# State-space block of a two-layer decoder: three pairs of states summed on GpSimd ahead of the matmul, rows spread two states ahead

## The chip, the cores and the metric

The kernel is one program on one core of one Trainium2 chip. The time is device microseconds of one execution. In the engine names of the profile PE is TensorE (PEld its weight loads), DVE is VectorE, ACT is ScalarE, POOL is GpSimd and SP is SyncE.

## The reference, cut to what matters

The model is a decoder of two layers on an input x of 32 batches x 112 positions x 256 channels. Its first block, the one that is changed, is a state-space block (Mamba). Everything behind it (cross attention, switch layer, agent attention, a second cross attention, latent mixture) is untouched. Cut to its core, in float32:

```python
x_in, z = split(layernorm(x) @ W_in)                  # 512 inner channels each
xc = silu(causal_conv4(x_in) @ pw + conv_bias)        # 4 taps
low = xc @ W_x                                        # 16 ranks, 8 B rows, 8 C rows
delta = softplus(low[:16] @ W_dt + b_dt)
for n in range(8):                                    # 8 states for each inner channel
    h[n] = scan over time of  exp(delta * A[n]) * h[n] + delta * B[n] * xc
y = sum over n of C[n] * h[n]  +  xc * D
x = x + (y * silu(z)) @ W_out
```

The sum over n of the eight products C[n] * h[n], which the kernel calls read-outs, is what the change computes in another way.

## The kernel before

The block runs in `mamba_groups`. The 32 batches go in eight groups of four; T = 448 positions of a group lie side by side, and the 512 inner channels are IC = 4 chunks of 128 partitions, so that most operands of VectorE are 128 x 1792. `all_groups` runs group 0, then a hardware loop over groups 1 to 5, then group 6 and, with `final=True`, group 7. Each engine has its own `group(g, at, final)` that goes through the states n = 0 to 7 in an order written out by hand; semaphores tie the engines together. While the states of group g are scanned, TensorE and ScalarE prepare group g+1.

VectorE, for a state: `scan(n)` (L664, state n from decay and drive), `make_drive(n+1)` (L657, delta*inner times the B row), `make_read_out(n)` (L671, state times the C row, into `read_out[:, n % 2]`). At state 6 it also runs `add_to_x(g, 0)` (L687, adds the projected output in PSUM to x), at state 7 `statistics` (L695). Behind state 7 come `make_delta(g+1)` (L649, L651), `make_drive(g+1, 0)`, `add_to_x(g, 1)`, `statistics` and `finish(g)` (L679, four products of y in PSUM with the gates).

TensorE, for a state n: `spread(g, n+1)` (L452, two bf16 matmuls that copy the B and the C row of state n+1 onto all 128 partitions, in `row_bank[0]` and `row_bank[1]`, one PSUM bank each), then the step of that state, then `add_state(g, n)` (L464), which waits for the read-out of state n and adds it to the four `y_bank` accumulators by matmuls with the identity. The steps are: n = 0 `gate` (L415), `turn_rows` (L408), `skip` (L458); n = 1 to 4 `convolve` (L427) of one chunk; n = 5 `low_rank` (L437) and `project_out(g, 0)` (L475); n = 6 `deltas` (L446); n = 7 a wait for `split`, `spread(g+1, 0)` and `project_out(g, 1)`. A float32 matmul stands as two records in the trace, so that `add_state` and `skip` are 8 records, a `convolve` 16.

ScalarE, for a state n: `keep_rows(n+1)` (L591, copies both row banks into `rows[:, (n+1) % 2]`, once the read-out of state n-1 has been made), then at n = 0 `read_gates` (L545) and `read_rows` (L540), then `decays(n+2)` (L598, four exponentials, once the scan of state n is done), then at n = 2 and 4 `read_inner` (L551), n = 3 `normalise_rows` (L534), n = 5 `read_low` (L558), n = 6 `cast_first` (L565) and `softplus` (L576 to L584, with `cast_second`, L570, in its midst), n = 7 `keep_rows(g+1, 0)` and `decays` of states 0 and 1 of the next group.

GpSimd has one job in this block: `split_low(g+1)`, two subtractions a group (L380 on 64 x 448 and L382 on 32 x 448), which make the exact bf16 parts of the rows. The second waits for `cast_second`.

## Time and profile before

| what | us |
|---|---|
| median of three runs | 3070.16 |
| range of the three | 3066.61 to 3071.97 |
| the profiled execution | 3073.5 |
| its span | 3071.7 |
| mean granted TensorE clock | 0.928 |

The page of the profile gives the busy time of each engine over the whole span and, in 40 slices of 77 us, the busy share of each engine in tenths. The state-space block fills slices 2 to 10 (some 80 to 785 us). For single instructions the timeline is read: start, duration, engine, line, output and inputs, and in brackets how long the engine had been idle before the instruction and which instruction released it. Instructions of VectorE that follow each other without a wait overlap a little in these records: a 1792-column product recorded at 2.02 us is followed by the next one 1.94 us after its start, a scan recorded at 3.88 us after 3.80 us.

### The profile page before, as it was taken

To read this page: it belongs to the slowest core of one execution; us is meant where nothing else is said; L and a number is where in the kernel's file an instruction comes from. 1 tells how busy PE (TensorE), PEld (TensorE's weight loads), DVE (VectorE), ACT (ScalarE), POOL (GpSimd) and SP (SyncE) were. 2 spreads that over 40 slices of the span, in tenths; PEclk is the share of its full clock that TensorE was granted. 3 is DMA by queue.
4 is the path that set the end of the run, shared out by engine and by line. 5 is a ranking of instruction groups with operands and counts; after the bars stand their busy time and mean duration, and the time that the engine had idled before them with its cause. 6 is when DMAs were issued, how large, how long until landed. Compare 5 with 4: busy or idle time off the path is not lost. (4 is left out here: it accounts for less than half of the span.)

```text
span 3071.7 us, 60127 instructions
## 1 busy us (share of the span) xinstructions
PE 2722.0 (89%) x20702; PEld 1767.6 (58%) x20703; DVE 1997.4 (65%) x4542; ACT 1518.1 (49%) x2982; POOL 454.4 (15%) x482
## 2 busy tenths in 40 slices
PE   6899999996799999999876689999999799969993
PEld 3344444443466676766665347777777645556662
DVE  2588888888367777777555447777777555653334
ACT  2666666663156666666443136666666233302222
POOL 0000000000300000000033111000110032324441
PEclk9899999997899999999877789999999899969997
DMA  4000000000100000000000100000000120001225
GB/s 112 0 1 0 0 0 0 0 0 0 35 21 20 20 15 20 20 20 15 1 15 1 39 11 26 20 20 20 20 25 11 49 83 20 14 26 61 63 61 165
DMA packets 57938, 80.70 MB, mean 26 GB/s; under 512 B 8880, under 2 KB 47059, under 8 KB 57491
## 3 DMA queue, kind: packets, MB, share of 16 engines
q1 hardware_dynamic: 51778, 62.69, 7.2%
q0 software_dynamic: 6048, 16.52, 1.7%
q8 instruction: 71, 1.16, 0.2%
q14 instruction: 41, 0.33, 0.0%
HBM read 63.59 MB, written 15.60 MB: 26 GB/s over the span
## 5 line engine op out<-in xcount | busy, mean ns | idle before, releaser
L1120 DVE CUSTOM_DVE_ANT_0 xa_h_scores<-xa_h_score_bank,xa_h_added 112x375 f32<-112x375 f32 x1024 | 518.1, 544 | 148.5 <-PE xa_h_score_bank L1055 133.6
L1214 ACT ACTIVATE xa_h_probs<-xa_h_scores,xa_h_negmax 112x375 f32<-112x375 f32 x1024 | 561.4, 600 | 0.9 <-DVE xa_h_negmax L1127 0.6
L1067 PEld LDWEIGHTS xa_h_turn_bank<-keep_ident,xa_h_probs 112*125 112x125 f32 x3072 | 398.6, 190 | 91.4 <-DVE xa_h_probs_t L1134 22.2
L1067 PE MATMUL xa_h_turn_bank<-keep_ident,xa_h_probs 112*125 112x112 f32 x3072 | 438.5, 279 | 8.8 <-DVE xa_h_probs_t L1134 8.5
L1134 DVE COPY xa_h_probs_t<-xa_h_turn_bank 125x448 f32<-125x448 f32 x512 | 319.1, 623 | 150.9 <-PE xa_h_turn_bank L1067 137.6
L1220 ACT ACTIVATE xa_h_probs_t<-xa_h_turn_bank 125x448 f32<-125x448 f32 x256 | 138.6, 541 | 304.5 <-PE xa_h_turn_bank L1067 304.5
L464 PE MATMUL mb_y_bank<-mb_read_out,keep_ident 128*128 128x448 f32 x512 | 231.7, 601 | 30.3 <-DVE mb_read_out L671 30.3
L664 DVE TENSOR_TENSOR_SCAN mb_state<-mb_decay,mb_drive 128x1792 f32<-128x1792 f32 x64 | 253.8, 3965 | 0.2 <-ACT mb_decay L598 0.2
L1055 PE MATMUL xa_h_score_bank<-xa_h_keys,xa_h_queries 32*112 32x375 f32 x2048 | 231.6, 522 | 11.3 <-DVE xa_h_row_max L1120 10.7
L1080 PEld LDWEIGHTS xa_h_sums_bank<-xa_h_probs_t,xa_h_values 125*32 125x32 f32 x6144 | 141.9, 110 | 154.5 <-DVE xa_h_probs_t L1134 149.2
L1080 PE MATMUL xa_h_sums_bank<-xa_h_probs_t,xa_h_values 125*32 125x112 f32 x6144 | 202.7, 265 | 14.6 <-issue 7.3
L1033 PE MATMUL xa_h_proj_bank<-xa_context,keep_slot 128*128 128x375 f32 x512 | 190.5, 495 | 12.0 <-POOL xa_h_added L1016 5.3
L1038 PE MATMUL xa_h_proj_bank<-keep_slot,xa_context 128*125 128x256 f32 x768 | 196.8, 393 | 4.4 <-ACT xa_h_values L1203 1.4
L427 PE MATMUL mb_front_bank<-mb_normed_t,mb_w_eff 128*128 128x448 f32 x512 | 198.9, 541 | 0.7 <-ACT mb_normed_t L540 0.7
L657 DVE TENSOR_TENSOR mb_drive<-mb_delta_inner,mb_rows 128x1792 f32<-128x1792 f32 x64 | 129.4, 2022 | 94.7 <-ACT mb_rows L591 93.8
L464 PEld LDWEIGHTS mb_y_bank<-mb_read_out,keep_ident 128*128 128x128 f32 x512 | 106.9, 212 | 140.6 <-issue 98.3
L2350 ACT ACTIVATE lm_e_wide<-lm_e_turn_bank,lm_b 128x128 f32<-128x128 f32 x252 | 71.8, 368 | 185.6 <-PE lm_e_turn_bank L2299 185.6
L591 ACT ACTIVATE mb_rows<-mb_row_bank 128x448 f32<-128x448 f32 x128 | 62.2, 537 | 190.7 <-PE mb_row_bank L452 190.7
L1038 PEld LDWEIGHTS xa_h_proj_bank<-keep_slot,xa_context 128*125 128x125 f32 x768 | 137.2, 192 | 28.8 <-DVE xa_heads_out L1147 6.7
L598 ACT ACTIVATE mb_decay<-mb_delta,mb_decay_rate 128x444 f32<-128x444 f32 x256 | 148.2, 657 | 5.9 <-DVE mb_delta L649 5.7
L427 PEld LDWEIGHTS mb_front_bank<-mb_normed_t,mb_w_eff 128*128 128x128 f32 x512 | 97.0, 190 | 89.9 <-issue 86.2
L671 DVE TENSOR_TENSOR mb_read_out<-mb_state,mb_rows 128x1792 f32<-128x1792 f32 x64 | 135.5, 2117 | 0.1
(341 smaller groups left out, 4145.7 us busy)
## 6 DMA issues: line engine op xcount, KB each, us to landing
xa_context<-in_ctx_t SPq DMA_DIRECT2D x64, 375.0 KB, 3.1
lm_w<-in_m_w SPq DMA_DIRECT2D x16, 512.0 KB, 9.9
lm_e_wide<-lm_result_rows SPq DMA_DIRECT2D x8, 896.0 KB, 9.8
keep_x<-in_x SPq DMA_DIRECT2D x4, 896.0 KB, 16.0
lm_latent_rows<-lm_rows SPq DMA_DIRECT2D x8, 448.0 KB, 3.2
out_x<-keep_x SPq DMA_DIRECT2D x8, 448.0 KB, 6.3
xa_mask_raw<-in_key_mask SPq DMA_DIRECT2D x1, 1312.5 KB
mb_f_pw<-in_pw SPq DMA_DIRECT2D x1, 1024.0 KB
```

The source lines that it names most:

```text
L427: last = pe.matmul(by_batch(bank[:, 0:T]), w_eff[:, tap, c, m * 128:(m + 1) * 128], normed_t[:, c, :, tap:tap + S], start=tap == 0 and c = ...
L464: last = pe.matmul(y_bank[c][:, 0:T], keep.ident[:, :], read_out[:, n % 2, c, :], start=False, stop=n == N - 1)
L598: last = act.activation(decay[:, n % 2, c, :, 1:], by_batch(delta[:, c, :])[:, :, 1:], ACT.Exp, scale=decay_rate[:, c, n:n + 1])
L664: dve.tensor_tensor_scan(flat(state[:, n % 2, :, :]), decay[:, n % 2, :, :, :].rearrange("p c b s -> p (c b s)"), flat(drive[:, n % 2, :, ...
L1033: last = pe.matmul(proj_bank[:, 0:SK], wk[:, c, m * 128:(m + 1) * 128], context[1 - s][:, c, :], start=c == 0, stop=c == DC - 1)
L1038: last = pe.matmul(proj_bank[0:KP, j * D:(j + 1) * D], context[1 - s][:, c, kc * KP:(kc + 1) * KP], wv[:, c, :], start=c == 0, stop=c == D ...
L1055: last = pe.matmul(score_bank[g][0:S, 0:SK], queries[s][band, m, j, :], keys[s][band, m, :], start=True, stop=True)
L1067: last = pe.transpose(turn_bank[(par + kc) % 2][0:KP, g * S:(g + 1) * S], probs[par][:, g, kc * KP:(kc + 1) * KP], keep.ident[0:S, 0:S])
L1080: last = pe.matmul(sums_bank[32 * g:32 * (g + 1), c * S:(c + 1) * S], values[s][:, kc, G * c + g, :], probs_t[par][:, kc, g * S:(g + 1) * ...
L1120: dve.tensor_tensor_reduce(scores[par][:, g, :], score_bank[g][0:S, 0:SK], added[s][:, :], 1.0, -BIG, ALU.add, ALU.max, row_max[par][:, g: ...
L1134: dve.tensor_copy(probs_t[par][:, kc, :], turn_bank[(par + kc) % 2][0:KP, 0:T]).then_inc(turned_by_dve, 1)
L1214: act.activation(probs[par][:, g, :], scores[par][:, g, :], ACT.Exp, bias=negmax[s][:, G * c + g:G * c + g + 1]).then_inc(probs_ready, 1)
```

## The change

Read-outs of the states 0+1, 2+3 and 4+5 are added on GpSimd (`add_pair`), and only the sum of a pair is pushed through TensorE; the states 6 and 7 are pushed singly as before. `read_out` has three buffers in place of two; a sum takes the place of one of its two operands. TensorE pushes the pair sums at n = 2, 4 and 6, ahead of which it does the step of that state and a spread. Rows are spread two states ahead (`spread(g, n+2)` at n; states 0 and 1 of the next group at n = 7), and a spread stands behind the step of the state, not ahead of it. `skip` moves from n = 0 to n = 1, behind the first `convolve`. On ScalarE `read_low` moves ahead of `decays(7)`. On GpSimd the three additions of a group stand ahead of `split_low`.

```diff
--- before.py
+++ after.py
@@ -313,7 +313,7 @@
         delta, delta_inner = sb("delta", [128, IC, T]), sb("delta_inner", [128, IC, T])
         decay = sb("decay", [128, 2, IC, G, S])
         drive, state = sb("drive", [128, 2, IC, T]), sb("state", [128, 2, IC, T])
-        read_out = sb("read_out", [128, 2, IC, T])
+        read_out = sb("read_out", [128, 3, IC, T])
         gated_y = sb("gated_y", [128, IC, T])
         y_bank = [psum(f"y_bank{n}", [128, 512]) for n in range(IC)]
         front_bank = [psum(f"front_bank{n}", [128, 512]) for n in range(2)]
@@ -331,6 +331,11 @@
         decay_ready, drive_ready, state_ready, read_out_ready, summed = (
             sem(n) for n in ("decay_ready", "drive_ready", "state_ready", "read_out_ready", "summed"))
         skipped, gated, x_added = sem("skipped"), sem("gated"), sem("x_added")
+        pair_ready = sem("pair_ready")
+        PAIRS = 3
+        PUSHES = N - PAIRS
+        BUFFER = (0, 1, 2, 0, 1, 2, 0, 2)
+        SUM = (1, 0, 1)
         LOADED = mamba_w.count
 
         def slots(g):
@@ -381,7 +386,15 @@
                 pool.wait_ge(parts_cast, 2 * g + 2)
                 pool.tensor_tensor(low_parts[0:LOW, :], rest[0:LOW, :], low_parts[0:LOW, :], ALU.subtract).then_inc(split, 1)
 
+            def add_pair(g, k):
+
+                pool.wait_ge(read_out_ready, N * g + 2 * k + 2)
+                pool.tensor_tensor(read_out[:, SUM[k], :, :], read_out[:, BUFFER[2 * k], :, :], read_out[:, BUFFER[2 * k + 1], :, :],
+                                   ALU.add).then_inc(pair_ready, 1)
+
             def group(g, at, final=False):
+                for k in range(PAIRS):
+                    add_pair(g, k)
                 if not final:
                     split_low(g + 1)
 
@@ -458,11 +471,19 @@
                     last = pe.matmul(y_bank[c][:, 0:T], skip_diag[:, c, :], inner[:, c, :], start=True, stop=False)
                 last.then_inc(skipped, 1)
 
-            def add_state(g, n):
+            def push(held, stop):
+
+                for c in range(IC):
+                    last = pe.matmul(y_bank[c][:, 0:T], keep.ident[:, :], read_out[:, held, c, :], start=False, stop=stop)
+                last.then_inc(summed, 1)
+
+            def push_pair(g, k):
+                pe.wait_ge(pair_ready, PAIRS * g + k + 1)
+                push(SUM[k], False)
+
+            def push_state(g, n):
                 pe.wait_ge(read_out_ready, N * g + n + 1)
-                for c in range(IC):
-                    last = pe.matmul(y_bank[c][:, 0:T], keep.ident[:, :], read_out[:, n % 2, c, :], start=False, stop=n == N - 1)
-                last.then_inc(summed, 1)
+                push(BUFFER[n], n == N - 1)
 
             def project_out(g, half):
 
@@ -485,15 +506,14 @@
             def group(g, at, final=False):
                 first = at == 0
                 for n in range(N):
-                    if n + 1 < N:
-                        spread(g, n + 1)
                     if n == 0:
                         gate(g)
                         if not final:
                             turn_rows(g)
-                        skip(g)
                     if 1 <= n < 5 and not final:
                         convolve(g, n - 1)
+                    if n == 1:
+                        skip(g)
                     if n == 5:
                         if not final:
                             low_rank(g)
@@ -505,7 +525,14 @@
                             pe.wait_ge(split, 2 * (g + 2))
                             spread(g + 1, 0)
                         project_out(g, 1) if not first else pass_over(OUT_B)
-                    add_state(g, n)
+                        if not final:
+                            spread(g + 1, 1)
+                    if n + 2 < N:
+                        spread(g, n + 2)
+                    if n in (2, 4, 6):
+                        push_pair(g, n // 2 - 1)
+                    if n >= 2 * PAIRS:
+                        push_state(g, n)
 
             pe.wait_ge(loaded, LOADED)
             pe.wait_ge(setup, 1)
@@ -517,6 +544,7 @@
             deltas(-1)
             pe.wait_ge(split, 2)
             spread(0, 0)
+            spread(0, 1)
             all_groups(pe, group)
             project_out(GROUPS, 0)
             project_out(GROUPS, 1)
@@ -606,6 +634,8 @@
                         read_gates(g)
                         if not final:
                             read_rows(g)
+                    if n == 5 and not final:
+                        read_low(g)
                     if n + 2 < N:
                         decays(g, n + 2)
                     if final:
@@ -616,8 +646,6 @@
                         normalise_rows(g + 2)
                     if n == 4:
                         read_inner(g, (2, 3))
-                    if n == 5:
-                        read_low(g)
                     if n == 6:
                         cast_first(g)
                         softplus(g)
@@ -666,13 +694,16 @@
 
             def make_read_out(g, n):
                 dve.wait_ge(row_read[1], use_of_row(g, 1, n) + 1)
-                reuse(dve, summed, N * g + n - 1)
+                if n in (3, 5, 7):
+                    reuse(dve, pair_ready, PAIRS * g + n // 2)
+                else:
+                    reuse(dve, summed, PUSHES * g + {0: -1, 1: -2, 2: 0, 4: 1, 6: 2}[n])
                 dve.wait_ge(state_ready, N * g + n + 1)
-                dve.tensor_tensor(read_out[:, n % 2, :, :], state[:, n % 2, :, :],
+                dve.tensor_tensor(read_out[:, BUFFER[n], :, :], state[:, n % 2, :, :],
                                   rows[:, n % 2, 1, :].unsqueeze(1).broadcast_to([128, IC, T]), ALU.mult).then_inc(read_out_ready, 1)
 
             def finish(g):
-                dve.wait_ge(summed, N * (g + 1))
+                dve.wait_ge(summed, PUSHES * (g + 1))
                 dve.wait_ge(front_read[(GATES + 2) % 2], used(g, GATES + 2) + 1)
                 dve.wait_ge(front_read[(GATES + 3) % 2], used(g, GATES + 3) + 1)
                 for c in range(IC):
```

## Rows read from the trace of the kernel before

**Rows 1.** The page: busy us of each engine, share of the span, instructions.
```profile
PE 2722.0 (89%) x20702; PEld 1767.6 (58%) x20703; DVE 1997.4 (65%) x4542; ACT 1518.1 (49%) x2982; POOL 454.4 (15%) x482
```

**Rows 2.** Groups by line, 80 to 780 us: busy, mean ns, idle before, releaser.
```profile
L657 DVE TENSOR_TENSOR mb_drive<-mb_delta_inner,mb_rows 128x1792 f32<-128x1792 f32 x64 | 129.4, 2022 | 94.7 <-ACT mb_rows L591 93.8
...
L591 ACT ACTIVATE mb_rows<-mb_row_bank 128x448 f32<-128x448 f32 x128 | 62.2, 537 | 190.7 <-PE mb_row_bank L452 190.7
```

**Rows 3.** Timeline, all engines, group 3, states 1 to 3 (start us, us, what).
```profile
366.62 2.33 ACT L598 ACTIVATE mb_decay<-mb_delta,mb_decay_rate 128x444 f32<-128x444 f32 x4
...
370.98 0.98 ACT L591 ACTIVATE mb_rows<-mb_row_bank 128x448 f32<-128x448 f32 x2 [2.03 <-PE mb_row_bank L452]
371.56 2.02 DVE L657 TENSOR_TENSOR mb_drive<-mb_delta_inner,mb_rows 128x1792 f32<-128x1792 f32 x1 [3.57 <-ACT mb_rows L591]
...
376.99 3.17 PE L464 MATMUL mb_y_bank<-mb_read_out,keep_ident 128*128 128x448 f32 x8
...
380.37 6.18 PE L427 MATMUL mb_front_bank<-mb_normed_t,mb_w_eff 128*128 128x448 f32 x16
...
380.96 2.03 DVE L657 TENSOR_TENSOR mb_drive<-mb_delta_inner,mb_rows 128x1792 f32<-128x1792 f32 x1 [1.64 <-ACT mb_rows L591]
...
386.39 3.17 PE L464 MATMUL mb_y_bank<-mb_read_out,keep_ident 128*128 128x448 f32 x8
```

**Rows 4.** Timeline, VectorE: state 2 of groups 0, 6; state 3 of group 7.
```profile
122.92 2.03 DVE L657 TENSOR_TENSOR mb_drive<-mb_delta_inner,mb_rows 128x1792 f32<-128x1792 f32 x1 [6.53 <-ACT mb_rows L591]
...
623.52 2.02 DVE L657 TENSOR_TENSOR mb_drive<-mb_delta_inner,mb_rows 128x1792 f32<-128x1792 f32 x1 [0.61 <-ACT mb_rows L591]
...
715.82 2.03 DVE L657 TENSOR_TENSOR mb_drive<-mb_delta_inner,mb_rows 128x1792 f32<-128x1792 f32 x1 [2.69 <-ACT mb_rows L591]
```

**Rows 5.** Timeline, GpSimd and VectorE, group 0, states 6 and 7.
```profile
173.43 3.88 DVE L664 TENSOR_TENSOR_SCAN mb_state<-mb_decay,mb_drive 128x1792 f32<-128x1792 f32 x1
...
173.69 4.44 POOL L382 TENSOR_TENSOR mb_low_parts<-mb_rest,mb_low_parts 32x448 bf16<-32x448 f32 x1 [2.06 <-ACT mb_low_parts L570]
...
177.44 2.58 DVE L671 TENSOR_TENSOR mb_read_out<-mb_state,mb_rows 128x1792 f32<-128x1792 f32 x1
```

**Rows 6.** Timeline, all engines, group 3, states 6 and 7.
```profile
416.84 0.66 DVE L687 TENSOR_TENSOR keep_x<-mb_front_bank,keep_x 112x512 f32 x1
...
421.67 2.85 DVE L671 TENSOR_TENSOR mb_read_out<-mb_state,mb_rows 128x1792 f32<-128x1792 f32 x1
...
424.42 1.02 POOL L382 TENSOR_TENSOR mb_low_parts<-mb_rest,mb_low_parts 32x448 bf16<-32x448 f32 x1 [1.78 <-ACT mb_low_parts L570]
424.44 4.75 DVE L664 TENSOR_TENSOR_SCAN mb_state<-mb_decay,mb_drive 128x1792 f32<-128x1792 f32 x1
424.57 6.29 PE L464 MATMUL mb_y_bank<-mb_read_out,keep_ident 128*128 128x448 f32 x8 [0.84 <-DVE mb_read_out L671]
...
428.48 1.79 ACT L584 ACTIVATE mb_soft<-mb_soft,keep_one 128x1792 f32<-128x1792 f32 x1
...
431.68 2.01 DVE L649 TENSOR_TENSOR mb_delta<-mb_above,mb_soft 128x1792 f32<-128x1792 f32 x1
```

**Rows 7.** Timeline, VectorE and GpSimd in the last block of the kernel.
```profile
2721.14 2.29 DVE L2441 TENSOR_TENSOR lm_e_wide<-keep_slot 112x2048 f32<-112x2048 f32 x1
2723.34 2.88 DVE L2439 TENSOR_TENSOR lm_e_own_tile<-keep_slot 112x1008 f32<-112x1008 f32 x1
...
2721.37 3.78 POOL L2252 TENSOR_TENSOR lm_e_own_tile<-lm_e_own_tile,keep_slot 112x1008 f32<-112x1008 f32 x1 [37.23 <-DVE lm_e_own_tile L2439]
```

**Rows 8.** Groups by line, GpSimd, whole span: the largest two-operand additions.
```profile
L794 POOL TENSOR_TENSOR keep_x<-keep_x,xa_out_bias 112x1024 f32<-112x1024 f32 x16 | 37.9, 2371 | 236.4 <-ACT xa_out_bias L843 192.9 <-DVE xa_q_normed L64 43.4
```

**Rows 9.** Timeline: GpSimd beside a VectorE instruction with a PSUM operand.
```profile
869.17 0.93 POOL L990 TENSOR_TENSOR xa_h_queries<-xa_queries_t,keep_slot 128x448 f32<-128x448 f32 x1 [25.65 <-PE xa_h_score_bank L1055]
869.31 0.55 DVE L1120 CUSTOM_DVE_ANT_0 xa_h_scores<-xa_h_score_bank,xa_h_added 112x375 f32<-112x375 f32 x1 [0.42 <-PE xa_h_score_bank L1055]
```

**Rows 10.** Windows: length, busy of PE, PEld, DVE, ACT, POOL; granted clock, DMA.
```profile
340.00:342.00 2.00, 2.00 (x4) 0.77 (x4) 2.00 (x1) 1.91 (x2) 0.47 (x1) 0.50 0.00 0
```

## The prediction

> **What bounds the kernel now.** I read the page first: TensorE is busy 89% of the span and VectorE 65% [rows 1], but that is a mean over stages, so the groups by line of the state-space block alone come next, and then the timeline of one group of it, engine by engine. In the block VectorE is the engine whose idle time means something. Its scans, drives and read-outs fill nearly all of it, and almost all that it waits for is one thing: the drive of the next state waits for the rows that ScalarE copies, 93.8 us in total, and ScalarE in turn has waited 190.7 us for the spread on TensorE [rows 2]. The timeline shows why. In states 2 to 5 TensorE pushes the read-out, spreads, and convolves without a break, and the next push starts 9.40 us after the last one (376.99 to 386.39); the push and the spread are 3.38 us of that (376.99 to 380.37), the convolution 6.02 (380.37 to 386.39) [rows 3]. VectorE needs only 3.80 + 1.94 + 1.93 = 7.67 us for a state, as consecutive starts go, and waits the rest, 1.64 us as recorded (1.73 with the overlap of records) [rows 3]. So TensorE's order sets the pace of four to five states, by its work and because a spread stands behind a push, and VectorE that of everything else.
>
> **What goes: pushes.** Three of eight pushes go. At some 3.0 us each (3.38 less some 0.38 for two bf16 matmuls of one pass) that is 9.0 us of TensorE's work a group. Two states then cost it 2 x 6.02 for convolutions, 3.0 for a push and 0.8 for spreads, 15.8 us, where VectorE needs 2 x 7.67 = 15.3 before anything is added. Alone, this would make the two about equal.
>
> **What goes: waits for rows.** A spread two states ahead is issued when the row bank has been read, which is as soon as read-out n-1 is made. ScalarE then copies (0.98 us) while the scan of 3.88 us runs, so the drive finds its rows. The recorded waits are 93.8 us over 47 drives; each is 0.09 more in true pace, 97.8 in total. One kind stays in part. At state 2 the copy also stands behind `decays(2)` on ScalarE, which ended at 368.95, while the copy began at 370.98: only 2.03 of that wait of 3.57 goes, because ScalarE is held by the gates before [rows 3]. Groups 2 to 5 keep 1.6 each, group 0 keeps 4.5 of its 6.53, while groups 1, 6 (0.61) and 7 have less than 2 to lose and lose it [rows 4]. That leaves 11.2. Removed: 97.8 - 11.2 = 86.6 us. What is late next is no longer rows but the port, below.
>
> **What comes: three additions a group on GpSimd, and who pays.** No addition of 128 x 1792 stands in the trace. The nearest is 112 x 1024 at 2.37 us (2.35 undisturbed) [rows 8], which is 2.29 ns a column; the 448-column one takes 1.02 us [rows 6], 2.28 ns. Both point at 1792 x 2.29 = 4.1 us. A price by the columns alone cannot be under 3.7 (0.93 x 4, from the cheaper form with a broadcast operand [rows 9]), nor do I see a reason for more than 4.4. GpSimd has time for it. But it doesn't work beside VectorE: in the trace the two exclude each other whenever VectorE's instruction has two SBUF operands. A GpSimd subtraction of 1.02 us issued just after a scan took 4.44 and ended only after the scan, which kept its 3.88; the read-out behind it grew from 2.02 to 2.58 [rows 5]. Where GpSimd came first, the scan grew from 3.88 to 4.75 and, two instructions before, the read-out from 2.02 to 2.85 [rows 6]. So VectorE loses what GpSimd takes, less some 0.17 us of start-up. It holds for a longer GpSimd instruction too: one that had to wait from 2721.37 to 2723.43 and then ran for 1.72 made VectorE's next one 2.88 us, where 1008 columns at the pace of 2.02 for 1792 would be 1.14 [rows 7]. An addition is released when the second read-out of its pair is made; by then the next scan holds the port, so the addition runs at the scan's end and the next drive waits for it. Price: 24 additions x (4.11 - 0.17) = 94.6 us.
>
> The Trainium skill ("SBUF — State Buffer", Who interferes with whom) says the same as a rule: a VectorE instruction with two SBUF inputs and a GpSimd instruction that reads SBUF take the shared port for a whole instruction, and the other blocks. It speaks against this change, and by that rule the trace agrees, as far as 1.7 us long ones show it. Its figure for a two-input addition of 2048 fp32 columns on GpSimd ("GPSIMD Engine Reference", Performance versus the Vector engine, 4497 ns) would give an estimate of 3.93 us for 1792, and a sum 4 us lower than mine.
>
> One part of the additions is covered: `add_to_x(g, 0)` at state 6 reads PSUM, and such an instruction isn't held up (0.55 us beside a running GpSimd product, its usual length) [rows 9]. It fits under the third addition in groups 1 to 7: 7 x 0.58 = 4.1 us given back [rows 6]. Without that cover the sum is 4.1 higher.
>
> **Moved steps, costed at nothing.** `split_low` is queued behind the third addition on GpSimd. Its L380 then gets the port behind drive 7, L382 behind the read-out of state 6; each delays VectorE by about 0.85 as now. `cast_second` on ScalarE waits for L380, and behind it are a quarter of the softplus, Exp and Ln. I follow it by VectorE's clock: Ln ends 2.4 us before `make_delta` is due; before, it ended at 430.27 with `make_delta` at 431.68, 1.4 us ahead [rows 6]. `skip` behind the first convolution fills time in which TensorE is not awaited. `read_low` ahead of `decays(7)` costs the scan of state 7 nothing, as there are two states of lead. The waits of read-outs 3, 5 and 7 for the addition two states back, and of read-out 4 for the first push (some 18 us earlier), end early. `finish` waits for the last push, which has the same work ahead of it as now. In group 7 the same account holds: drives there wait 2.69 [rows 4].
>
> **The sum.** -86.6 + 94.6 - 4.1 = +3.9 us. The span of 3071.7 becomes 3075.6, the profiled execution's 3073.5 becomes 3077.4. That execution lies 3.3 above the median of 3070.16; on the median's scale the forecast is 3074. Seen for one group: from the drive at 371.56 to that at 623.52 three groups pass, the last of them shorter by 3.57 - 0.61 of waiting, so a group takes (251.96 + 2.96) / 3 = 85.0 [rows 3, 4]. Less its waits for rows (3.66, four of 1.73, 2.28: 12.9) and 1.7 for `split_low`, VectorE's own pace is 70.4. Afterwards: 70.4 + 1.7 + 1.65 (state 2) + 3 x 3.94 - 0.6 = 85.0 again. The gain of TensorE and the loss of VectorE cancel. The bounds of an addition, 3.7 and 4.4, move the sum by -10 and +7.
>
> **The rivals.** (a) The port is shared more kindly in long instructions, or additions hide: if VectorE lost nothing, 3070 - 87 = 2983. For it speaks only that no addition of 4 us has been seen; against it every collision in the trace. A milder form has the gates step at the full clock in all groups, so that the 11.2 us that stay go too: 3063. Together 0.13.
> (b) The softplus chain becomes late (slower): `cast_second` waits for L380, which waits for the third addition and a drive. If L380 gets its turn one instruction later (the read-out, 1.9 us) and TensorE's `deltas` are late as well, Ln ends behind the read-out of state 7, and VectorE waits before `make_delta`. The point is 2.4 us of lateness; 1.5 to 2.5 us beyond it in seven groups is +10 to +17, so about 3088. The slack of 1.4 us of today speaks for it, the order of the port (who waits gets it next) against. 0.12.
> (c) TensorE's clock. It now waits some 3 us ahead of each push of a pair. After waits of this kind its granted clock is 0.50, the 1.2 GHz level [rows 10], and a push takes 6.29 in place of 3.17 [rows 6]. It has 19.3 - 15.8 = 3.5 us to spare in two states, so it becomes the bound once over 7 us of each 19.3 run at half speed; the stretches of now are under that. At 10 us it costs 1.5 us in each of 21 pairs, 3105. 0.06.
> (d) The change doesn't do what it says: rows still come late, and the 94.6 are added alone, 3160. ScalarE's 2.03 us of idleness ahead of the copy, until TensorE, speaks against [rows 3]. 0.03.
>
> **How the numbers follow.** The forecast case has 0.66 and its own range is 3062 to 3085. About 0.2%, 6 us, is what a measurement of this kernel can tell from no change. Within the case the sum lies inside 3064 to 3076 with 0.46, above with 0.15, below with 0.05. With (a) 0.13 faster, (b) 0.12, (c) 0.06 and (d) 0.03 slower, and rounding (a)'s milder form partly into "same": faster 0.17, same 0.47, slower 0.36. The range takes in the bounds of the addition and most of (b): 3060 to 3092.
>
> **What would show it.** The additions stand on GpSimd with about 4.1 us of their own, recorded at up to 8 as they wait for a scan. The drive behind scans 2, 4 and 6 takes some 6 us in place of 2.02, with no idle time before it. Drives of states 3 to 7 wait for no rows; that of state 2 waits some 1.6 in groups 2 to 5. A group still takes 85 us. TensorE's busy time falls by up to 70 us, with more of it at 0.50. I am wrong if drives keep their 2.02 us (then it is much faster), if `make_delta` stands behind a wait for Ln, or if `finish` waits for a push.

## The result, and the profile after

| | us |
|---|---|
| changed kernel, median of 10 runs | 3060.26 (3059.38 to 3067.24) |
| kernel before, 10 runs | 3070.51 (3064.97 to 3073.68) |
| ratio, with its 95% interval | 0.9972 (0.9963 to 0.9981) |
| profiled execution after, its span | 3060.0, 3057.6 |

The changed kernel is faster by 10 us, 0.28%, where the forecast was 3.9 us slower. The page of the changed kernel first; its columns are those of [rows 1]:

```profile
PE 2667.0 (87%) x20510; PEld 1736.8 (57%) x20511; DVE 2078.2 (68%) x4542; ACT 1519.2 (50%) x2982; POOL 644.4 (21%) x506
```

TensorE has 55 us less work, VectorE is recorded busy 81 us longer with the same number of instructions, and GpSimd has the 24 additions. The groups by line, changed kernel, 80 to 780 us (busy, mean ns, idle before, releaser), answer to [rows 2]:

```profile
L685 DVE TENSOR_TENSOR mb_drive<-mb_delta_inner,mb_rows 128x1792 f32<-128x1792 f32 x64 | 213.6, 3338 | 15.5 <-ACT mb_rows L619 14.7
L392 POOL TENSOR_TENSOR mb_read_out<-mb_read_out 128x1792 f32<-128x1792 f32 x24 | 179.7, 7489 | 446.7 <-DVE mb_read_out L702 446.7
L619 ACT ACTIVATE mb_rows<-mb_row_bank 128x448 f32<-128x448 f32 x128 | 61.7, 532 | 79.7 <-DVE mb_read_out L702 32.3 <-issue 26.6 <-PE mb_row_bank L465 20.8
```

The drive's idle time has fallen from 94.7 to 15.5 us, and its busy time has grown from 129.4 to 213.6: two numbers of nearly the same size with opposite signs. In the timeline of group 3, states 1 to 4, the exchange is seen in one place (changed kernel; VectorE and GpSimd; answers to [rows 3]):

```profile
371.36 2.03 DVE L685 TENSOR_TENSOR mb_drive<-mb_delta_inner,mb_rows 128x1792 f32<-128x1792 f32 x1 [2.56 <-ACT mb_rows L619]
...
375.24 3.88 DVE L692 TENSOR_TENSOR_SCAN mb_state<-mb_decay,mb_drive 128x1792 f32<-128x1792 f32 x1
...
375.40 7.50 POOL L392 TENSOR_TENSOR mb_read_out<-mb_read_out 128x1792 f32<-128x1792 f32 x1 [34.12 <-DVE mb_read_out L702]
...
379.04 5.74 DVE L685 TENSOR_TENSOR mb_drive<-mb_delta_inner,mb_rows 128x1792 f32<-128x1792 f32 x1
...
390.44 1.99 DVE L685 TENSOR_TENSOR mb_drive<-mb_delta_inner,mb_rows 128x1792 f32<-128x1792 f32 x1
```

The addition begins 0.16 us into the scan, ends at 382.90, 3.78 us after the scan's end at 379.12, and the drive behind the scan is recorded at 5.74 us in place of 2.02. The drive of the next state, with no addition beside it, has 1.99 and no wait for rows. At states 6 and 7 of the same group (changed kernel, VectorE and ScalarE; answers to [rows 6]):

```profile
417.14 0.66 DVE L718 TENSOR_TENSOR keep_x<-mb_front_bank,keep_x 112x512 f32 x1
417.72 5.14 DVE L685 TENSOR_TENSOR mb_drive<-mb_delta_inner,mb_rows 128x1792 f32<-128x1792 f32 x1
422.78 2.85 DVE L702 TENSOR_TENSOR mb_read_out<-mb_state,mb_rows 128x1792 f32<-128x1792 f32 x1
425.55 4.72 DVE L692 TENSOR_TENSOR_SCAN mb_state<-mb_decay,mb_drive 128x1792 f32<-128x1792 f32 x1
...
428.49 1.79 ACT L612 ACTIVATE mb_soft<-mb_soft,keep_one 128x1792 f32<-128x1792 f32 x1
...
432.76 2.01 DVE L677 TENSOR_TENSOR mb_delta<-mb_above,mb_soft 128x1792 f32<-128x1792 f32 x1
```

`add_to_x` is hidden under the third addition, and Ln ends at 430.28, 2.48 us ahead of `make_delta`.

So the block does what the forecast said, and it gains nothing. The first scan starts at 104.3 us (before: 104.9), and the statistics' aggregation right behind the block (its first instruction outside) at 785.5 (before: 785.8; second profiles of both kernels, below, have it at 787.3 and 784.5, so the block's length is known to some 3 us). The 14.1 us by which the two profiled spans differ are 0.3 up to there and 13.8 behind it, in blocks that the change doesn't touch. Cut by the first instructions of each block in the timelines:

| stretch behind the block | before | after |
|---|---|---|
| up to the first attention's heads | 56.2 | 56.2 |
| its 8 heads | 664.5 | 660.0 |
| its output projection | 46.3 | 45.0 |
| agent attention | 245.3 | 243.9 |
| second attention: heads, output | 650.3 | 650.4 |
| latent attention | 260.4 | 255.3 |
| last block | 362.9 | 361.4 |

Two things make these differences. The first is a stall of TensorE in the latent attention that has no releaser. In the timeline it stands ahead of one pair of products, in the kernel before:

```profile
2580.65 0.70 PE L1915 MATMUL lm_a_query_banks<-lm_a_keys_wide,lm_a_queries 32*112 32x448 f32 x2 [3.75 <-issue]
```

and in the changed kernel at the same product:

```profile
2569.63 0.63 PE L1946 MATMUL lm_a_query_banks<-lm_a_keys_wide,lm_a_queries 32*112 32x448 f32 x2 [0.39 <-issue]
```

The second is TensorE's granted clock. The windows of the first heads have the same instructions in both kernels but another busy time of TensorE (length; busy of PE, PEld, DVE, ACT, POOL; granted clock, DMA); first the kernel before:

```profile
842.00:1506.50 664.50, 635.50 (x6592) 454.49 (x6593) 469.82 (x1507) 412.14 (x865) 50.35 (x64) 0.98 0.06 18
```

then the changed kernel:

```profile
841.70:1501.60 659.90, 630.04 (x6592) 450.52 (x6592) 469.80 (x1507) 412.42 (x865) 50.46 (x64) 0.99 0.06 18
```

Most of the 5.5 us of busy time lie at the end of the stretch, as the timeline shows. In the kernel before the last turns of a head run at half speed, with the clock at its 1.2 GHz level:

```profile
1491.64 0.84 PE L1080 MATMUL xa_h_sums_bank<-xa_h_probs_t,xa_h_values 125*32 125x112 f32 x24 [1.03 <-DVE xa_h_probs_t L1134]
1492.41 3.08 PE L1067 MATMUL xa_h_turn_bank<-keep_ident,xa_h_probs 112*125 112x112 f32 x12
```

and in the changed kernel, two rows for the same 12 turns, at 2.4 GHz:

```profile
1489.93 0.78 PE L1111 MATMUL xa_h_sums_bank<-xa_h_probs_t,xa_h_values 125*32 125x112 f32 x24 [1.03 <-DVE xa_h_probs_t L1165]
1490.65 1.12 PE L1098 MATMUL xa_h_turn_bank<-keep_ident,xa_h_probs 112*125 112x112 f32 x8
1492.05 0.69 PE L1098 MATMUL xa_h_turn_bank<-keep_ident,xa_h_probs 112*125 112x112 f32 x4 [0.28 <-DVE xa_h_probs_t L1165]
```

The engine had done the same before in both, with the same wait of 1.03 us ahead of the products. The trace's record of the clock, summed from the block's end to the kernel's end, has 320 us at the lower level before and 299 after. Half of 21 us is some 10 us of TensorE's work, an estimate that fits what the stages lost beside the stall.

### The profile page after: what moved, and what is told of

Its sections match the earlier page's. It is cut to its first block and busy times, and to the rows that moved or that the text cites. A ratio compares the mean times of both kernels' runs of the same rounds, so it can differ in the third digit from the quotient of the medians.

```text
span 3057.6 us, 59832 instructions
## 1 busy us (share of the span) xinstructions
PE 2667.0 (87%) x20510; PEld 1736.8 (57%) x20511; DVE 2078.2 (68%) x4542; ACT 1519.2 (50%) x2982; POOL 644.4 (21%) x506
## 5 line engine op out<-in xcount | busy, mean ns | idle before, releaser
L392 POOL TENSOR_TENSOR mb_read_out<-mb_read_out 128x1792 f32<-128x1792 f32 x24 | 179.7, 7489 | 446.7 <-DVE mb_read_out L702 446.7
L1086 PE MATMUL xa_h_score_bank<-xa_h_keys,xa_h_queries 32*112 32x375 f32 x2048 | 231.0, 520 | 11.5 <-DVE xa_h_row_max L1151 10.7
L685 DVE TENSOR_TENSOR mb_drive<-mb_delta_inner,mb_rows 128x1792 f32<-128x1792 f32 x64 | 213.6, 3338 | 15.5 <-ACT mb_rows L619 14.7
L1111 PE MATMUL xa_h_sums_bank<-xa_h_probs_t,xa_h_values 125*32 125x112 f32 x6144 | 201.4, 264 | 14.7 <-issue 6.1
L477 PE MATMUL mb_y_bank<-mb_read_out,keep_ident 128*128 128x448 f32 x320 | 162.5, 666 | 44.3 <-POOL mb_read_out L392 43.4
L440 PEld LDWEIGHTS mb_front_bank<-mb_normed_t,mb_w_eff 128*128 128x128 f32 x512 | 96.3, 189 | 96.1 <-issue 93.8
L477 PEld LDWEIGHTS mb_y_bank<-mb_read_out,keep_ident 128*128 128x128 f32 x320 | 73.6, 237 | 126.7 <-issue 73.2
## 6 DMA issues: line engine op xcount, KB each, us to landing
keep_x<-in_x SPq DMA_DIRECT2D x4, 896.0 KB, 15.5
```

The costliest lines, as they stand in the source:

```text
L440: last = pe.matmul(by_batch(bank[:, 0:T]), w_eff[:, tap, c, m * 128:(m + 1) * 128], normed_t[:, c, :, tap:tap + S], start=tap == 0 and c = ...
L477: last = pe.matmul(y_bank[c][:, 0:T], keep.ident[:, :], read_out[:, held, c, :], start=False, stop=stop)
L685: dve.tensor_tensor(drive[:, n % 2, :, :], delta_inner[:, :, :], rows[:, n % 2, 0, :].unsqueeze(1).broadcast_to([128, IC, T]), ALU.mult).t ...
L1086: last = pe.matmul(score_bank[g][0:S, 0:SK], queries[s][band, m, j, :], keys[s][band, m, :], start=True, stop=True)
L1111: last = pe.matmul(sums_bank[32 * g:32 * (g + 1), c * S:(c + 1) * S], values[s][:, kc, G * c + g, :], probs_t[par][:, kc, g * S:(g + 1) * ...
```

## The experiments

All runs in one table. "Block" is the start of the aggregation behind the block, "rest" the time from there to the end, and "low" the part of the rest in which the clock was at 1.2 GHz, all from the profiled execution, a single one that can lie several us beside the median; "stall" is the idle time ahead of the product in the latent attention. The expectations below count "low" otherwise: they give 312 to 325 us for the kernel before and 292 to 306 for the changed one, where the clock records between the block's end and the kernel's end sum to 320 and 299.

| kernel | median | ratio to before, 95% | block | rest | low | stall |
|---|---|---|---|---|---|---|
| before | 3070.51 | | 785.8 | 2286.0 | 320 | 3.75 |
| changed | 3060.26 | 0.9972 (0.9963 to 0.9981) | 785.5 | 2272.1 | 299 | 0.39 |
| no_pair | 3040.47 | 0.9910 (0.9893 to 0.9926) | 756.7 | 2281.0 | 312 | 3.6 |
| one_pair | 3031.87 | 0.9880 (0.9864 to 0.9897) | 750.4 | 2275.7 | 299 | 0.4 |
| two_pairs | 3056.26 | 0.9951 (0.9934 to 0.9968) | 770.5 | 2282.8 | 330 | 0.4 |
| middle_pair | 3053.41 | 0.9945 (0.9928 to 0.9961) | 772.4 | 2279.0 | 316 | 0.4 |
| rows_one_ahead | 3061.41 | 0.9965 (0.9949 to 0.9981) | 785.4 | 2280.9 | 318 | 0.4 |
| half_addition | 3013.59 | 0.9805 (0.9789 to 0.9821) | 736.0 | 2275.6 | 299 | 0.4 |
| before_padded | 3077.67 | 1.0018 (1.0008 to 1.0027) | 796.1 | 2281.1 | 318 | 0.4 |
| changed_padded | 3098.37 | 1.0067 (1.0045 to 1.0089) | 812.0 | 2284.6 | 319 | 3.6 |
| before_repeated | 3071.97 | 1.0001 (0.9991 to 1.0011) | 784.5 | 2285.8 | 323 | 3.6 |
| changed_repeated | 3062.24 | 0.9968 (0.9955 to 0.9980) | 787.3 | 2272.6 | 300 | 0.4 |
| before_delayed | 3070.69 | 0.9995 (0.9985 to 1.0004) | 786.4 | 2281.2 | 322 | 3.6 |
| before_delayed_twice | 3069.00 | 1.0003 (0.9993 to 1.0012) | 788.8 | 2279.8 | 314 | 3.5 |
| before_delayed_4_times | 3072.59 | 1.0009 (1.0000 to 1.0019) | 793.6 | 2276.3 | 303 | 3.7 |
| changed_delayed | 3068.61 | 0.9993 (0.9983 to 1.0002) | 786.2 | 2275.6 | 296 | 0.4 |
| changed_delayed_twice | 3069.99 | 1.0004 (0.9995 to 1.0014) | 791.5 | 2277.4 | 315 | 0.4 |
| changed_delayed_4_times | 3071.09 | 1.0010 (1.0001 to 1.0020) | 795.4 | 2281.7 | 319 | 0.4 |

The kernel before, on the same chip, had a median of 3070.22 beside no_pair, one_pair, two_pairs and rows_one_ahead; 3072.14 beside half_addition, the padded kernels and before_repeated; 3071.84 beside the single delays, middle_pair and changed_repeated; and 3068.91 beside the delays by two and four.

### How many pairs

Three kernels take one part of the change each: the spreads two states ahead, the third buffer and the moved steps stay, and none, one (states 0 and 1) or two pairs are added on GpSimd. In no_pair the read-outs of states 0 and 1 are pushed together at n = 1. The edit of one_pair, for all three with other tables:

```diff
-        PAIRS = 3
+        PAIRS = 1
...
-        BUFFER = (0, 1, 2, 0, 1, 2, 0, 2)
+        BUFFER = (0, 1, 2, 0, 1, 2, 0, 1)
...
-                    if n in (2, 4, 6):
-                        push_pair(g, n // 2 - 1)
-                    if n >= 2 * PAIRS:
-                        push_state(g, n)
+                    for kind, m in PUSHED.get(n, []):
+                        (push_pair if kind == "p" else push_state)(g, m)
```

> The changed kernel without its additions: all eight read-outs are pushed singly, three buffers, rows spread two states ahead. Port theory (each addition costs VectorE 3.7 us, 24 of them): VectorE's own pace is then 70.4 + 1.7 + 1.7 = 74 us a group, TensorE's work with all pushes about the same, plus its waits for the gates and deltas; a group takes 78 to 81 us where the changed kernel takes 85.3, about 3020 us in all, and the drives of states 2 to 5 wait for no rows or little. Rival, TensorE's work sets the pace and the additions cost nothing: with 9 us more pushes a group this is slower than the changed kernel, 3070 to 3130.

> Only the states 0+1 are added on GpSimd, the other six are pushed singly, rows two states ahead. Port theory: 74 + 3.7 = 77.7 us a group on VectorE, TensorE at 71 of work plus waits just under it, so 77.5 to 79 us a group and about 3005 us in all. Rival (TensorE's work sets the pace): slower than the changed kernel by the two pushes of 3 us a group that come back, 3065 to 3110.

> States 0+1 and 2+3 are added on GpSimd, four are pushed singly, rows two states ahead. Port theory: 74 + 2 x 3.7 = 81.4 us a group, 3.7 less than the changed kernel in each of eight: about 3031 us. Rival (TensorE's work sets the pace): one push of 3 us a group more, 3062 to 3085.

All three are 20 to 27 us slower than the port theory said (3040.5 for 3020, 3031.9 for 3005, 3056.3 for 3031). It counted VectorE's own pace and took the waits for nearly gone; they are not, as the lines below show, and in two_pairs the rest of the program is besides 10.7 us longer than in the changed kernel.

By the block's end the change falls into steps: 785.8, without pairs 756.7 (-29.1), with one 750.4 (-6.3), with two 770.5 (+20.1), with three 785.5 (+15.0). A pair costs VectorE 8 x 3.72 = 29.8 us in eight groups; what it brings is the waits that it takes away. VectorE's waits from 100 us to the block's end (us in total, times, longest), in no_pair:

```profile
DVE mb_drive L685 <- ACT mb_rows L619: 56.2, 31, 3.4
DVE keep_x L719 <- PE mb_front_bank L498: 14.3, 9, 3.8
```

in one_pair:

```profile
DVE keep_x L719 <- PE mb_front_bank L498: 18.0, 9, 5.5
DVE mb_drive L685 <- ACT mb_rows L619: 16.1, 17, 2.6
```

and in two_pairs:

```profile
DVE mb_delta L677 <- ACT mb_soft L612: 68.5, 7, 48.9
DVE keep_x L719 <- PE mb_front_bank L498: 11.9, 4, 5.5
DVE mb_drive L685 <- ACT mb_rows L619: 8.3, 6, 2.6
```

The first pair removes 40 us of waits for rows for its 29.8, the second 8 of rows and 6 ahead of `add_to_x`, while the wait for the softplus grows (68.5, of which 48.9 is the one at the start of the block; in one_pair 60.0 and 48.8). The third costs 15.0 and not 29.8, as under it the softplus is waited for at the start of the block alone (47.7): the addition takes the place of that wait. From one pair on, VectorE has little left to win. one_pair is faster than both kernels, by 1.2% than the kernel before.

middle_pair tests whether it matters which pair is added: states 2 and 3 in place of 0 and 1, the states 0 and 1 pushed together at n = 1.

```diff
+        FIRST = 2
...
-                pool.wait_ge(read_out_ready, N * g + 2 * k + 2)
+                pool.wait_ge(read_out_ready, N * g + FIRST + 2)
```

> One pair again, but the states 2+3 in place of 0+1; the others are pushed singly. By the port theory a group costs VectorE the same as with states 0+1 (one addition of 3.7 us), so 80 us a group and 3032 within 8 us. It would be faster only if TensorE, which is behind from state 3 on with the pair 0+1, is relieved at a better place; slower if the two single pushes at state 1 delay the convolutions.

It matters, where the expectation had 3032: 3053.41 against 3031.87, the block 22.0 us longer. The waits in middle_pair's block:

```profile
DVE mb_delta L678 <- ACT mb_soft L613: 75.9, 7, 47.8
DVE mb_drive L686 <- ACT mb_rows L620: 34.5, 12, 4.2
DVE keep_x L720 <- PE mb_front_bank L499: 10.8, 3, 5.5
```

16 us more of the softplus and 18 more of rows than in one_pair, with 7 less ahead of `add_to_x`. Why the softplus and the rows come later with this pair is open.

### Rows one state ahead

> The changed kernel with all its three additions, but rows spread one state ahead and at the head of each state's step, as before the change. Port theory: with three pushes gone and VectorE slowed by the port TensorE is early anyway, a spread at the head of a step is in time, and the result stays at 3060 within 8 us; only the drive of state 2 may wait 2 us longer in some groups. Rival, the waits for rows went because of the longer lead: they come back at 1.7 us for each of five states in eight groups, 3100 to 3130.

```diff
                 for n in range(N):
+                    if n + 1 < N:
+                        spread(g, n + 1)
...
-                        if not final:
-                            spread(g + 1, 1)
-                    if n + 2 < N:
-                        spread(g, n + 2)
```

VectorE's waits over the block, rows_one_ahead:

```profile
DVE mb_drive L682 <- ACT mb_rows L616: 14.6, 6, 4.1
```

The same six waits as in the changed kernel (14.7, 6, 4.2), and the block ends at 785.4 against 785.5. With three pairs the lead of the spreads brings nothing: TensorE has so little left that one state ahead is early enough. The profiled rest was 2280.9 with no stall, against 2272.1 in the changed kernel, though the block ends 0.1 us apart; its five runs lay between 3052.04 and 3068.32, and the profiled one was the slowest of them. That was the first sign that the rest moves by itself.

### Half an addition

> The changed kernel, but the additions on GpSimd cover only the first two of the four chunks of channels (896 columns of 1792), so that the sums of the other two lack one state of each pair. Everything else, pushes and waits, is the same. Port theory: an addition holds the port half as long, about 1.95 us, so that the drive behind it is recorded at some 3.9 us in place of 5.7, a group takes 3 x 1.85 = 5.5 us less and the block about 44 us less; 3060 becomes about 3018. Rival, VectorE waits for something else at those places (the semaphore of a pair, TensorE): the drives keep 5.7 and the time stays.

```diff
-                pool.tensor_tensor(read_out[:, SUM[k], :, :], read_out[:, BUFFER[2 * k], :, :], read_out[:, BUFFER[2 * k + 1], :, :],
+                pool.tensor_tensor(read_out[:, SUM[k], 0:2, :], read_out[:, BUFFER[2 * k], 0:2, :], read_out[:, BUFFER[2 * k + 1], 0:2, :],
```

The addition covers two of the four chunks, 896 of 1792 columns; in the other two a sum lacks one of its states. The timeline of half_addition, group 3:

```profile
357.79 5.60 POOL L392 TENSOR_TENSOR mb_read_out<-mb_read_out 128x896 f32<-128x896 f32 x1 [32.98 <-DVE mb_read_out L702]
...
361.43 3.85 DVE L685 TENSOR_TENSOR mb_drive<-mb_delta_inner,mb_rows 128x1792 f32<-128x1792 f32 x1
...
370.94 1.99 DVE L685 TENSOR_TENSOR mb_drive<-mb_delta_inner,mb_rows 128x1792 f32<-128x1792 f32 x1
```

The drive loses 3.85 - 1.99 = 1.86 us, half of the 3.75 (5.74 - 1.99) under a whole addition, and the block ends 49.5 us earlier: 24 x 1.87 = 45, and most of the rest is less waiting for rows (10.0 us against 14.7). VectorE pays for each column that GpSimd adds, at 2.1 ns, with nothing fixed on top that these two sizes show. This is the port theory of the prediction, confirmed by size.

### The stall in the latent attention

> The kernel before with 96 idle instructions on TensorE ahead of the block. If the stall in the latent attention goes by the place in the program, it goes here and 5 us with it: 3065. Rival: no difference, 3070.

> The changed kernel with 189 idle instructions (semaphore increments that nobody waits for) ahead of the state-space block on TensorE, while it waits for the weights: its instructions behind the block then stand as far along in the program as in the kernel before, which has 189 more. Theory that the 10 us went in untouched blocks, by two ways: the block itself ends at 785 as before, and the stall of TensorE without a named cause in the latent attention (3.8 us in the kernel before, 0.4 in the changed one), if it goes by the place in the program, comes back, which is worth 5 us: some 3065. Rival, the gain comes from the block or its data: no difference, 3060.

```diff
+            for _ in range(96):
+                pe.sem_inc(padding, 1)
             pe.wait_ge(loaded, LOADED)
             pe.wait_ge(setup, 1)
```

(189 in place of 96 in changed_padded.) Idle instructions ahead of TensorE's part of the block move every later instruction of its program and change nothing else in it. TensorE's waits in the latent attention that end in no releaser (us in total, times, longest), in before_repeated:

```profile
PE lm_a_query_banks L1915 <- issue: 3.6, 1, 3.6
```

in before_padded:

```profile
PE lm_a_query_banks L1918 <- issue: 0.4, 1, 0.4
```

and in changed_padded:

```profile
PE lm_a_query_banks L1949 <- issue: 3.7, 2, 3.6
```

The stall goes from the kernel before and comes back in the changed one, and the stage follows: 255.4 us in before_padded and 260.1 in changed_padded, against 260.4 and 255.3. So the stall goes by the place of the instructions in TensorE's program; no_pair, which has as many pushes as the kernel before, has it too. It is not the time at which they run: the delays below leave it where it was in both kernels.

The traces also show what TensorE does in it. Between the product before the stall and the stalled one it jumps back to the head of the stage's loop (L1810 in the kernel before). The jumps of the loop's two turns, by source line (shortest, median and longest ns, first and last start), in the kernel before, the changed kernel and changed_padded:

```profile
L1810 PEldq COMPARE_BRANCH  x2: 83/1828/3572, 2576.7 to 2640.3; - x2
...
L1841 PEldq COMPARE_BRANCH  x2: 76/144/211, 2569.0 to 2627.7; - x2
...
L1844 PEldq COMPARE_BRANCH  x2: 83/1708/3332, 2602.7 to 2666.1; - x2
```

While the long jump runs (kernel before, 2576.7 to 2580.3), the DMA engines move a packet of the queue that carries instructions:

```profile
q8 instruction: 1, 0.02, 2.1%
```

In all seven traces with the stall the jump takes 3.3 to 3.6 us, and a packet of 16 KB of that queue starts 1.0 us into it. In the eleven without the stall the same jump takes 0.21 us and no such packet runs beside it. The reading that fits is that TensorE waits there for its own instructions to be loaded; that rests on this coincidence in 18 traces and was not tested by itself. Behind the stall the kernel before loses a little more: its clock is at 1.2 GHz for the next 3.4 us, where the changed kernel's stays at 2.4.

As a price the padding is dear: the idle instructions start 0.15 us apart in the trace, and the first scan starts 9.9 us later with 96 idle instructions (114.8 against 104.9) and 25.0 later with 189, which is why both padded kernels are slower.

### The clock behind the block

> The kernel before, unchanged: a second profile, to see what differs between two executions of one program. The state-space block should end at 785 to 786 again and the stall in the latent attention should stand at 3.8 us; the time TensorE's clock spends at its lower level in the untouched blocks (325 us in the first profile of before, 306 in that of after) may differ, and the rest of the program with it, by up to 8 us.

> The changed kernel, unchanged: a second profile. The block ends at 785.5 within 1 us again; no stall above 1 us in the latent attention. If the shares of the rest go by the program, everything behind the block takes 2272 us again; if they go by how each execution falls against TensorE's clock, anything from 2270 to 2283.

Both repeat: 2285.8 and 2272.6 us of rest, as in the first profiles, and 3071.97 and 3062.24 as medians. So the 10 us are not chance between single runs. Next a pure delay, one to four products on VectorE as the last instructions of the block, of which nothing uses the result:

```diff
             for half in range(2):
                 add_to_x(GROUPS, half)
                 statistics(GROUPS, half)
+            dve.tensor_tensor(flat(delta[:, :, :]), flat(delta_inner[:, :, :]), flat(delta_inner[:, :, :]), ALU.mult).then_inc(delta_ready, 1)
```

(For two and four, a wait for the one before stands between them.) TensorE's program is the same instruction for instruction.

> The kernel before with the same extra product as the last instruction of its block: 2.0 us later at the block's end. If the time of the untouched blocks depends on where they fall against the steps of TensorE's clock, the rest moves from its 2286 by up to 9 us in either direction, most likely down; if it is fixed, 3070 + 2 = 3072. The stall in the latent attention should stay (3.6 to 3.8 us), since TensorE's program isn't touched.

> The changed kernel with one more product of 128 x 1792 on VectorE as the last instruction of the state-space block (its result is not used): the block ends 2.0 us later, everything behind is the same code in the same places of the other engines' programs. Theory that the untouched blocks' time depends on where their waits fall against the steps of TensorE's clock: the rest of the program (2272 us in the profile) moves by something else than nothing, up to +9 or -2 us, and the time with it. Rival, it is fixed: 3060 + 2 = 3062.

> The kernel before with the same two products. Start time decides: at some delay the kernel before gives back 5 us or more, so that its time grows by less than the 4 us or even falls. It stays with the program: rest 2290 (2286.0 plus the delay), lower-clock time 312 us, kernel about 3075.

> The kernel before with four products, about 8 us. Start time decides: rest less the delay other than 2286 by several us. It stays with the program: rest 2294, lower-clock time 312 us, kernel about 3079.

> The changed kernel with two extra products of VectorE as the last instructions of the block, about 4 us of pure delay. The time from the block's end to the kernel's end was 2272.1 us in the changed kernel and 2286.0 in the kernel before, 2282.0 without the TensorE stall. If the start time of the later blocks decides, that time less the delay of about 4 us lands anywhere between 2271 and 2282 and the lower-clock time anywhere between 287 and 320 us, other than in the undelayed kernel by more than 2 us at some of the delays tried. If it stays with the program, the rest is 2276 (2272.1 plus the delay), the lower-clock time 292 us, and the kernel's time about 3066.

> The same with four products, about 8 us. Start time decides: rest less the delay between 2271 and 2282, not steadily 2272. It stays with the program: rest 2280, lower-clock time 292 us, kernel about 3070.

The block's end as measured lies behind the added products (784.5 to 787.3 without them, 793.6 and 795.4 with four), so the rest doesn't hold the delay, and the last four expectations are to be read without it: the theory that it stays with the program says 2286 and 2272 at every delay. The profiled executions say, at 0, 1, 2 and 4 products: kernel before 2285.9, 2281.2, 2279.8, 2276.3; changed kernel 2272.3, 2275.6, 2277.4, 2281.7. Each of these is one execution, and with a delay the executions of one program spread more than before: those of changed_delayed lie between 3062.66 and 3078.01, and the profiled one of changed_delayed_4_times was the slowest of its ten. An estimate for the typical execution is the median of the spans less the block's end in the profile: kernel before 2285.7, 2282.5, 2278.4, 2277.2; changed kernel 2272.4, 2279.8, 2276.6, 2273.7. The kernel before gets quicker with the delay; the changed one gets slower by 7 us with one product and comes most of the way back with four. The windows of the first heads show what a profiled execution can have, with the sides exchanged; before_delayed_4_times:

```profile
849.20:1508.80 659.60, 630.03 (x6592) 450.54 (x6593) 469.73 (x1507) 412.39 (x865) 50.50 (x64) 0.99 0.06 18
```

and changed_delayed_4_times:

```profile
852.80:1517.90 665.10, 635.79 (x6592) 454.62 (x6592) 469.55 (x1507) 412.12 (x865) 50.34 (x64) 0.98 0.06 18
```

In the medians, changed less before at the same delay is -10.3 and -9.6 (no product, two comparisons), -2.1 (one), +1.0 (two) and -1.5 (four). Both kernels of a delay ran on one chip. The stall stays on its side in all six delayed kernels, so that some 5 us of advantage are in these differences too: the clock's part turns from -5 to about +3 to +6. So the theory that the rest stays with the program falls: the later blocks are quicker or slower by up to 10 us by when they start, with TensorE's clock at its lower level for another time, and the changed kernel happens to start them well.

Part of how it keeps to that place so steadily (nine of its ten first runs lie between 3059.38 and 3062.03) is in the clock records. The clock last falls 0.08 us ahead of the block's end in both profiles of the kernel before, and 0.55 and 0.54 us ahead of it in both of the changed kernel: the block ends at a fixed place against a step of the clock, each kernel at its own, and one product moves it to 2.02 and 2.50. It is not the whole of it. In rows_one_ahead the clock falls 0.56 us ahead of the block's end, and the stretch up to the first heads and the heads take 57.9 and 665.3 us there, 56.2 and 660.0 in the changed kernel. What makes that difference is open.

## Why the prediction was wrong

**What bounds the kernel, and the port: right.** VectorE and TensorE set the block's pace, VectorE loses what GpSimd takes, `add_to_x` hides under the third addition (5.14 in place of 5.74 for the drive, 7 x 0.60 = 4.2 us, forecast 4.1), and the drive behind an addition takes "some 6 us", 5.74. The rivals (a), (b) and (d) did not happen, (b) least: Ln is 2.48 us ahead, where 2.4 was said. Of (c), the clock did fall more (176 us at 1.2 GHz from the first scan to the block's end, 94 before), but TensorE did not become the bound. That (a) in its milder form names 3063 is luck: the waits it would have removed stayed.

**The addition: mis-sized by 6%.** A drive lost 3.72 us and not 3.94, 24 times, 5.3 us in all. The addition ran 3.78 us, not 4.11; the columns at 2.29 ns, taken from smaller instructions, were too dear, and the lower bound of 3.7 was nearer. The Trainium skill's figure ("GPSIMD Engine Reference", Performance versus the Vector engine), from which the prediction worked out an estimate of 3.93, was nearer than the value taken, and this trace is below both.

**The waits at state 2: mis-sized the other way.** 14.7 us of waits for rows stay, in six drives, where 11.2 were forecast; that of group 3 is 2.56, not 1.54. The wait for `add_to_x`'s bank fell by some 2 us (11.0 to 9.3) and was not in the sum. A slip of 0.2 us is in the sum as well: 93.8 + 47 x 0.09 is 98.0, not 97.8.

**The block's sum: right within its bounds.** Forecast +3.9, measured -0.3; the groups take 83.9 to 85.3 us from first scan to first scan where 85 was forecast, and the seventh 82.4 (before: 82.0). Removed and added cancel, and the errors above nearly do too. The experiments correct the reading of the first number, though. The prediction gave the waits to the pair of measures, spreads and pushes; no_pair shows that the spreads, the third buffer and the moved steps alone take 29 us off the block (which of them, no run takes apart), and rows_one_ahead that under three pairs the lead takes nothing. The pairs are not the price of the gain; the second and the third are a loss of 20.1 and 15.0 us, which the sum of all parts could not show.

**The step that failed is the one that stands nowhere in the sum: that everything behind the block costs the same.** "The sum is made against its own time", the block's +3.9 was added to 3073.5 and scaled to the median, and 2286 us of other blocks were carried over unchanged. They lost 13.8 us in the two profiles, 10 in the medians. About 5 of it (3.4 of stall, the latent attention 5.1 shorter) is the stall that the removed instructions shifted away, shown by padding in both directions. The rest, 9 us in the profiles and some 5 in the medians, goes with TensorE's clock: it is at 1.2 GHz for 21 us less, 3.4 of them behind the stall, and the delays show that the same instructions take another time when they start at another time. The prediction looked at the clock inside the block alone (rival c), and as a loss. That this term exists could be seen before: the product with 3.75 us of idleness and no releaser stands in the trace of the kernel before, and its three runs spread over 5 us with one and the same program. Neither tells the sign. That the range of 3060 to 3092 holds 3060.26, at its very edge, is luck: its lower bound came from the price of an addition, and the 10 us came from elsewhere. The chances by sign, with 6 us as the mark, should have carried a spread of 5 to 10 us around the block's sum, to both sides.

## What to carry to other kernels

When an edit moves work from one engine to another under a shared port, time its parts alone before all together: here one pair of three and the wider spreads are 38 us faster than the kernel before (35 of them in the block), and the whole change 10 (none in the block). When a change leaves its own block as long as it was and the kernel's time moves by 0.3%, cut the two traces at the block's end first, and before crediting the edit, repeat it with a delay of a few us: at two and four products of delay the difference of 10 us between these kernels was +1.0 and -1.5. A sum of a block's rows can't promise a kernel's time more closely than the rest of the program moves by itself, some 10 us here.

## What the runs showed of the hardware

TensorE's jump back in the loop of the latent attention took 3.3 to 3.6 us in seven traces, each with a 16 KB packet of the instruction queue that started 1.0 us into it, and 0.21 us in eleven traces without such a packet. 96 idle instructions ahead of it in the kernel before took the stall away, and 189 in the changed kernel brought it back: it goes by the place in the program, not by time.

2280 us of identical instructions took up to 10 us more or less with delays of 2 to 8 us ahead of them: between 296 and 330 us of the rest ran at 1.2 GHz in the traces, and ten executions of one delayed program lay up to 15 us apart. 96 semaphore increments on TensorE delayed the block by 9.9 us and 189 by 25.0; they start 0.15 us apart.

VectorE's loss beside GpSimd was proportional to the columns added at the two sizes run (1.86 us for 896, 3.75 for 1792). The Trainium skill ("SBUF — State Buffer", Who interferes with whom) describes the port as locked for a whole instruction; that was seen before for up to 1.7 us of a running instruction, and holds here for 3.78.
